# Graph-network kernel on one core: the attention stage's run masks are made once, ahead of it, and loaded per block

## The chip, the cores and the metric

One core of one Trainium2 chip runs the whole program. The metric is the device time of one execution in microseconds (us). The engines are named as in the profile: PE (TensorE), DVE (VectorE), ACT (ScalarE), POOL (GpSimd) and SP (SyncE, here only a queue that issues transfers).

## The reference, cut to what matters

Four graph layers follow one another, each with a residual and a layer norm. The change is in the fourth, an attention layer over 200,000 edges that are sorted by their target node:

```python
h = x @ W
alpha = h[dst] @ wa[:c] + edge_attr @ wa[c:c + ce] + h[src] @ wa[c + ce:]
alpha = jnp.where(alpha > 0, alpha, NEG_SLOPE * alpha)
m = jax.ops.segment_max(alpha, dst, num_segments=n)
a = jnp.exp(alpha - m[dst])
s = jax.ops.segment_sum(a, dst, num_segments=n)
out = jax.ops.segment_sum((a / (s[dst] + 1e-16))[:, None] * h[src], dst, num_segments=n) + bias
```

`dst` is sorted, so the edges of one node are a run of neighbours. The maximum over a node's edges is a running maximum that starts anew at the head of each run and is read at its last element. That needs two masks for each edge: is it the head of a run (then a term of -1e30 is added to what was carried along), and is it the last of a run (then its value is kept).

## The kernel before, in words

**Tiling.** The 6,250 nodes are 49 blocks of 128. The edges of one target block `d` lie in 49 cells of up to 128 edges, one for each source block. A cell is a column of [128, 49] tiles, or a row of [49, 128] tiles after a transpose. An earlier stage writes to DRAM the one-hot matrices of the edges' ends (`OND`, `OSD`), the dense 6250 x 6250 adjacency `AD` and, in `ROWS3`, the local source and target numbers of each cell.

**Stages.** After a first stage of some 1,240 us come the *dense passes* (`passes_*`): twice through the 49 rows of `AD`, 1.57 MB each, through three buffers, with 49 matmuls a row. POOL has no code there. Then come `pairs3_*`, the third layer, and `pairs4_*`, the attention stage. Each engine's order is what the code writes; semaphores alone tie the engines together.

**The attention stage** is a software pipeline of 343 steps `t` (7 for each block, `G` = 7), and 42 more to drain. `due4(t, off)` gives the step that work with an offset is due for, `block4(t, off)` the block when one begins. In each step:

- PE multiplies 7 cells of one-hot sources by node rows (L1668), ACT copies the result to `H` (L1606).
- ACT scales 7 cells by the attention weights (L1627, seven activations: the *values*) into one of four buffers `V4`. DVE subtracts the bf16 part (L1817), POOL subtracts the next one (L1655: the *look*). PE adds up the three parts (L1688). ACT may fill the buffer again after that.
- DVE makes one-hot rows of loaded target numbers (L1755) and source numbers (L1750), each every second step.

Once in each block there is a chain through all engines that finds the maxima:

- PE transposes the block's target numbers (L1695) into `ps[2]`; ACT copies them to `dcol` in `MISC` (L1613).
- POOL makes the masks of them in four dependent instructions on [49, 128]: difference to the neighbour (L1646), equal or not (L1648), `negs` (L1650) and `lastf` (L1651). They stand in POOL's order between two looks, so the next look waits for them.
- DVE scans with `negs` (L1841) and multiplies by `lastf` (L1843). PE transposes the product and `lastf` (L1708, L1709). DVE splits it (L1849 to L1854), PE spreads it to the edges (L1719), DVE finds the maximum of each node (L1859 to L1872), PE collects it (L1678), DVE makes the exponents (L1807 to L1813) and ACT the exponential (L1617).

Every seventh block begins a layer norm of seven finished blocks, one DVE instruction (L1771 to L1796) in each of 14 steps.

SP issues the loads: sources (L1546), targets (L1552, which wait for PE's L1678 of a block since that frees their buffers) and one-hot matrices (L1564).

Of the kernel before, what the change touches and what calls it, by code (L numbers as in the profile page):

```python
# [53 lines left out]
def gnn_kernel(nc, x, src, dst, eattr, ew, ew2, W1n, b1n, W1r, Wl1, bl1, W2n, b2n, W2r, Wl2, bl2,  # L54
               W2g, b2g, dcoef, cpar, spar, W3, watt, bias3, out):
    with ExitStack() as ctx:
# [1167 lines left out]
        def pairs3_sp(sp):  # L1224
# [14 lines left out]
            sp.wait_ge(row_mm.at, 2 * NB)  # L1239
            for n in range(4):  # L1240
# [256 lines left out]
        seg, negs, lastf, ylast = (Tflat[0:NB, 1225 + 130 * n:1225 + 130 * n + w] for n, w in enumerate((129, P, P, P)))  # L1497
# [19 lines left out]
        dtr, dcp, flg, sgk = on(cat_t, NB), on(cat_ev, NB), on(cat_d, NB), on(t_out, NB)  # L1517
# [73 lines left out]
        def pairs4_act(act):  # L1591
# [6 lines left out]
            for t in range(LASTT):  # L1598
                d, g, k = due4(t, 1)
                if k is not None:  # L1600
                    act.wait_ge(hg.at, hg.o + k + 1)
# [885 lines left out]
```

## Time and profile before

| | |
|---|---|
| median of 3 runs | 3592.72 us (3590.33 to 3595.03) |
| profiled execution | 3591.77 us, of which the span of its instructions 3590.0 us |
| PE / DVE / ACT / POOL busy, share of the span | 81% / 81% / 62% / 44% |
| first pass over `AD`, second pass | 1241 to 1461 us, 1461 to 1712 us |
| attention stage, from the first block's exponents to the last one's | 2717.7 to 3556.9 us |
| granted TensorE clock, mean | 0.94 of full speed |

A line of a group gives the line of the code, the engine, what is written and read, and the time. A time in brackets is idle time just ahead of an instruction, with what ended it. The busy time of an engine includes time in which an instruction has started and is held up, so a long duration of an instruction that is short elsewhere is itself a wait.

### The profile page before, as it was taken

What the parts mean: (1) busy time and instruction counts of PE and PEld (TensorE: products, weight loads), DVE (VectorE), ACT (ScalarE), POOL (GpSimd) and SP (SyncE); (2) the same over time, 40 slices, a digit from 0 to 9 for tenths busy, and PEclk for the clock granted to TensorE, in tenths of its full rate; (3) what the DMA queues carried; (4) which work ended last, traced back from release to release, by engine and by line L of the source; (5) the groups of instructions that cost most, each with busy time, mean ns of one, the idle gap of its engine ahead of it and who ended that gap; (6) DMA issues with size and microseconds to landing.
All of it is one profiled execution on the core that took longest, in us unless ns stands there. A gap on an engine that the chain in (4) does not pass through costs nothing.

```text
span 3590.0 us, 122167 instructions
## 1 busy us (share of the span) xinstructions
PE 2911.7 (81%) x50473; PEld 2637.4 (73%) x50473; DVE 2904.2 (81%) x4610; ACT 2219.8 (62%) x6003; POOL 1584.4 (44%) x1253
## 2 busy tenths in 40 slices
PE   0199999999999699899688888787768888888886
PEld 0178888888888599899677777777757777777775
DVE  7599999999999522233688888898857999999997
ACT  6334444444444400001698888898857898899887
POOL 2012222222221000000399988898964655666564
PEclk9999999999999899999899999999977888888887
DMA  8157777777777799898687877787738888888884
GB/s 221 66 157 244 237 232 234 243 237 231 234 243 236 253 370 360 330 328 320 215 279 259 264 264 248 254 271 250 257 124 302 279 278 277 276 290 274 267 278 129
DMA packets 606666, 907.43 MB, mean 253 GB/s; under 512 B 358505, under 2 KB 494858, under 8 KB 587163
## 3 DMA queue, kind: packets, MB, share of 16 engines
q1 hardware_dynamic: 583992, 800.62, 68.1%
q10 hardware_dynamic: 19763, 94.38, 7.1%
q8 instruction: 406, 6.65, 0.7%
q0 software_dynamic: 2352, 4.52, 0.3%
q14 instruction: 153, 1.25, 0.1%
HBM read 651.96 MB, written 247.40 MB: 251 GB/s over the span
## 4 chain that ended last, share of the span: by engine, by line
PE 36%; DVE 27%; ACT 14%; issue 10%; POOL 6%; DMA 5%; ACTq 1%; SPq 0%; DVEq 0%; POOLq 0%
PE ps L683 9%; PE ps L1047 8%; PE ps L709 4%; DMA U<-AD 4%; ACT U L1627 3%; POOL EDG L1268 3%; DVE EDG L1755 3%; DVE U L1817 3%; PE ps L696 3%; ACT U L569 3%; POOL EDG L1260 2%; ACT U L1329 2%; PE ps L667 2%; PE ps L1289 1%; DVE A L1389 1%
## 5 line engine op out<-in xcount | busy, mean ns | idle before, releaser
L569 ACT ACTIVATE U<-ps 128x512 bf16<-128x512 f32 (+1 forms) x637 | 356.4, 573 | 499.5 <-PE ps L696 475.5
L1627 ACT ACTIVATE U<-U,T 128x65 f32<-128x65 f32 x1806 | 460.1, 343 | 47.7 <-PE ps L1688 42.3
L1260 POOL TENSOR_TENSOR EDG<-U,edge 128x512 f32<-128x512 f32 (+1 forms) x196 | 214.3, 1098 | 584.1 <-DVE edge L1412 551.1
L1047 PE MATMUL ps<-U 128*128 128x192 bf16 x4802 | 418.5, 248 | 33.2 <-DMA U<-AD 32.8
L1047 PEld LDWEIGHTS ps<-U 128*128 128x128 bf16 x4802 | 402.8, 98 | 42.5 <-DMA U<-AD 39.2
L1655 POOL TENSOR_TENSOR U<-U 128x455 f32<-128x455 f32 x258 | 296.4, 1152 | 215.3 <-DVE U L1817 215.3
L866 DVE TENSOR_TENSOR EDG<-edge,EDG 128x1792 bf16<-128x1792 bf16 x343 | 367.5, 1083 | 14.4 <-DMA OSD<-EDG 12.0
L502 POOL DMA_INDIRECT U<-REC,nod x49 | 94.0, 1918 | 622.4 <-PE ps L638 501.2
L683 PE MATMUL ps<-U 128*128 128x98 bf16 (+1 forms) x5292 | 363.5, 223 | 4.5 <-DVE U L854 3.5
L709 PE MATMUL ps<-EDG,U 128*128 128x193 bf16 x2401 | 311.4, 249 | 51.1 <-ACT U L569 39.9
L683 PEld LDWEIGHTS ps<-U 128*128 128x128 bf16 x5292 | 341.3, 98 | 15.7 <-DVE U L854 11.9
L1296 PE MATMUL ps<-U 128*128 128x65 bf16 x7203 | 287.2, 195 | 72.3 <-DVE A L1389 71.8
L1270 POOL TENSOR_TENSOR EDG<-EDG 128x896 f32<-128x896 f32 (+1 forms) x172 | 312.4, 1817 | 13.5
L1268 POOL TENSOR_TENSOR EDG<-EDG 128x896 f32<-128x896 f32 (+1 forms) x172 | 308.6, 1794 | 11.7 <-ACT EDG L1348 11.7
L1296 PEld LDWEIGHTS ps<-U 128*128 128x128 bf16 x7203 | 252.1, 98 | 80.5 <-DVE A L1389 80.1
L1289 PE MATMUL ps<-U 128*128 128x65 bf16 x7203 | 289.6, 195 | 13.8 <-ACT U L1331 8.0
L1389 DVE TENSOR_TENSOR A<-ps,U 128x455 f32<-128x455 f32 x343 | 210.4, 622 | 95.7 <-ACT U L1339 77.0
L1289 PEld LDWEIGHTS ps<-U 128*128 128x128 bf16 x7203 | 271.3, 98 | 18.5 <-issue 10.1
L1348 ACT ACTIVATE EDG<-U,edge 128x64 f32<-128x64 f32 x1029 | 279.3, 338 | 9.0 <-PE ps L1308 6.1
L1139 DVE TENSOR_REDUCE A<-ps 128x64 f32<-128x192 f32 x98 | 34.3, 355 | 294.3 <-PE ps L1047 294.0
L854 DVE TENSOR_TENSOR U<-U 128x3920 bf16<-128x3920 bf16 (+1 forms) x132 | 263.7, 2000 | 0.0
L1381 DVE TENSOR_SCALAR U<-U,iotap 128x1792 bf16<-128x1792 bf16 x228 | 252.7, 1109 | 1.5 <-DMA U<-ROWS 1.5
(323 smaller groups left out, 7019.4 us busy)
## 6 DMA issues: line engine op xcount, KB each, us to landing
U<-ROWS SPq DMA_DIRECT2D x411, 448.0 KB, 4.7
U<-AD SPq DMA_DIRECT2D x98, 1568.0 KB, 8.6
OND<-EDG SPq DMA_DIRECT2D x343, 224.0 KB, 2.8
OSD<-EDG SPq DMA_DIRECT2D x343, 224.0 KB, 3.6
AD<-U ACTq DMA_DIRECT2D x49, 1568.0 KB, 5.6
EDG<-ROWS SPq DMA_DIRECT2D x171, 448.0 KB, 6.3
U<-OND SPq DMA_DIRECT2D x303, 224.0 KB, 5.9
U<-OSD SPq DMA_DIRECT2D x213, 224.0 KB, 4.7
```

Of the source, the lines that this page charges most:

```text
L569: ev4.by(act.activation(prow[i % NPW][:, P * g:P * (g + m)], ps[4 + gg % 2][:, 0:P * m], ACT.Copy))
L683: ins = pe.matmul(ps[3][:, o:o + NB * (f1 - f0)], w_, FR[h][:, c, f0:f1, :, k], start=(h + c + k + f0 == 0), stop=(last and f0 == 0))
L709: ins = pe.matmul(ps[6][:, 0:XW], prow[i % NPW][:, P * j:P * j + P], Xs[:, j, :], start=(j == 0), stop=(j == NB - 1))
L866: hot8.by(dve.tensor_tensor(HOT[r].rearrange("p s c (r k) -> p (s c) r k", k=2), bc(r1v.unsqueeze(1), [P, 14, D, 2]), bc(sdb[i % 2][:, b, ...
L1047: ins = pe.matmul(ps[q][:, 0:192], arow[r][:, P * j:P * j + P], (XsB if p else XsA)[:, j, :, :].rearrange("p s f -> p (s f)"), start=(j == ...
L1260: ins = pool.tensor_tensor(VD[:, v:v + w, 0, KA * D:G * D].rearrange("p w (k f) -> p w k f", f=D), W_, bc(c_.unsqueeze(3), [P, w, G - KA, ...
L1268: rem3.by(pool.tensor_tensor(VD[:, v:v + w, 1, :], VD[:, v:v + w, 0, :], VH[:, v:v + w, 0, :], ALU.subtract))
L1270: low3.by(pool.tensor_tensor(VD[:, v:v + w, 2, :], VD[:, v:v + w, 1, :], VH[:, v:v + w, 1, :], ALU.subtract))
L1289: ins = pe.matmul(ps[h][:, 65 * k:65 * k + 65], rw[r][:, 2 * P * k + P:2 * P * k + 2 * P], Ws[:, i0 + k, s_, 0:65], start=(s_ == 0), stop= ...
L1296: ins = pe.matmul(ps[2 + h][:, 65 * k:65 * k + 65], rw[r][:, 2 * P * k:2 * P * k + P], Ws[:, j, s_, 0:65], start=(s_ == 0), stop=(s_ == 2))
L1627: ins = act.activation(V4[k % NV][:, 0, c, :], H[k % NHR][:, c, :], ACT.Copy, scale=a4[d % 2][:, s:s + 1])
L1655: look.by(pool.tensor_tensor(V4[k % NV][:, 2, :, :], V4[k % NV][:, 1, :, :], S4[k % NV][:, 1, :, :], ALU.subtract))
```

## The change

The masks don't depend on the layers' values, only on the edges' targets. So POOL now makes them in the dense passes (`passes_pool`), for seven target blocks in one go. SP first loads all target numbers into `EDG` (49 x 49 cells of 128 numbers of two bytes, 0.61 MB), ahead of the first row of `AD`. POOL makes both masks in bf16 in `EDG`; SP stores them to a DRAM tensor `MSK` in the second pass, seven stores, each ahead of the last row of `AD` of a group. In the attention stage SP loads `MSK[d]` (49 rows of 512 bytes) into one of two buffers `masks`, behind a wait that the block two before has been read. The four POOL instructions, the ACT copy and the PE transpose of each block are gone, with their waits. The transpose of `lastf` is now a bf16 matmul with an identity. `GV` and `GR` are empty, so `value_at` and `rest_at` wait as before.

```diff
+        def passes_pool(pool):
+            msk_d.by(pool.memset(mdif[:, :, 0:1], 1.0))
+            msk_d.by(pool.memset(mdif[:, :, P:P + 1], 1.0))
+            pool.wait_ge(msk_ld.at, msk_ld.o + 16)
+            for g in range(NGB):
+                bl = slice(GB * g, GB * g + GB)
...
+                msk_d.by(pool.tensor_tensor(mdif[:, :, 1:P], mdst[:, bl, 1:P], mdst[:, bl, 0:P - 1], ALU.subtract))
+                pool.wait_ge(msk_d.at, msk_d.o + 4 * g + 3)
+                msk_d.by(pool.tensor_scalar(mdif, mdif, 0.0, 1.0, ALU.is_equal, ALU.subtract))
+                pool.wait_ge(msk_d.at, msk_d.o + 4 * g + 4)
+                msk_ok.by(pool.tensor_scalar(mboth[:, bl, 0, :], mdif[:, :, 0:P], BIG, None, ALU.mult))
+                msk_ok.by(pool.tensor_scalar(mboth[:, bl, 1, :], mdif[:, :, 1:P + 1], -1.0, None, ALU.mult))
+            pool.wait_ge(msk_st.at, msk_st.o + 16 * NGB)
+
         def passes_sp(sp):
+            msk_ld.by(sp.dma_start(mdst, ROWS3[1].rearrange("d (s r) -> s d r", r=P)), 16)
             for p in range(2):
                 for i in range(NB):
                     r = i % NA
+                    if p and i % GB == GB - 1:
+                        g = i // GB
+                        sp.wait_ge(msk_ok.at, msk_ok.o + 2 * g + 2)
+                        msk_st.by(sp.dma_start(MSK[GB * g:GB * g + GB].rearrange("d s m r -> s d (m r)"),
+                                               mboth[:, GB * g:GB * g + GB, :, :].rearrange("p d m r -> p d (m r)")), 16)
...
+            def run_masks(d):
+
+                if d >= 2:
+                    sp.wait_ge(ytr.at, ytr.o + d - 1)
+                mk_ld[d % 2].by(sp.dma_start(masks[d % 2], MSK[d]), 16)
+
             sp.wait_ge(att.at, NGB)
             nt = 0
+            run_masks(0)
+            run_masks(1)
...
+                d = block4(t, 2)
+                if d is not None and d >= 2:
+                    run_masks(d)
...
         def pairs4_act(act):
...
-                d = block4(t, 6)
-                if d is not None:
-                    act.wait_ge(dtr.at, dtr.o + d + 1)
-                    if d:
-                        act.wait_ge(flg.at, flg.o + 2 * d)
-                    dcp.by(act.activation(dcol, ps[2][0:NB, P:2 * P], ACT.Copy))
...
         def pairs4_pool(pool):
             for t in range(LASTT):
-                d = block4(t, 7)
-                if d is not None:
-                    pool.wait_ge(dcp.at, dcp.o + d + 1)
...
-                    sgk.by(pool.tensor_tensor(seg[:, 1:P], dcol[:, 1:P], dcol[:, 0:P - 1], ALU.subtract))
-                    pool.wait_ge(sgk.at, sgk.o + 2 * d + 1)
-                    sgk.by(pool.tensor_scalar(sege, seg, 0.0, 1.0, ALU.is_equal, ALU.subtract))
-                    pool.wait_ge(sgk.at, sgk.o + 2 * d + 2)
-                    flg.by(pool.tensor_scalar(negs, sege[:, 0:P], BIG, None, ALU.mult))
-                    flg.by(pool.tensor_scalar(lastf, sege[:, 1:P + 1], -1.0, None, ALU.mult))
                 d, g, k = due4(t, 18)
...
         def pairs4_pe(pe):
...
-                    dtr.by(pe.transpose(ps[2][0:NB, P:2 * P], E3v[:, d, :, 1], ident[:, :]))
...
-                    ytr.by(pe.transpose(ps[3][:, 64:64 + NB], lastf, ident[0:NB, 0:NB]))
+                    ytr.by(pe.matmul(ps[3][:, 64:64 + NB], masks[d % 2][:, 1, :], identh, start=True, stop=True))
...
         def pairs4_dve(dve):
...
-                    dve.wait_ge(flg.at, flg.o + 2 * d + 2)
-                    dvf.by(dve.tensor_tensor_scan(ysc, negs, ps[2][0:NB, 0:P], -BIG, ALU.add, ALU.max))
+                    dve.wait_ge(mk_ld[d % 2].at, mk_ld[d % 2].o + 16 * (d // 2 + 1))
+                    dvf.by(dve.tensor_tensor_scan(ysc, masks[d % 2][:, 0, :], ps[2][0:NB, 0:P], -BIG, ALU.add, ALU.max))
...
+                passes_pool(pool)
                 pairs3_pool(pool)
```

On POOL, in the middle of the attention stage, two blocks stand in a row like this before. `U<-U` and `MISC<-MISC` are looks, the 49-row instructions make masks:

```order
L1655 TENSOR_TENSOR U<-U 128x455 x3
L1655 TENSOR_TENSOR MISC<-MISC 128x455
L1646 TENSOR_TENSOR T<-MISC 49x127
L1648 TENSOR_SCALAR MISC<-T 49x129
L1650 TENSOR_SCALAR T<-MISC 49x128
L1651 TENSOR_SCALAR T<-MISC 49x128
L1655 TENSOR_TENSOR U<-U 128x455 x3
L1655 TENSOR_TENSOR MISC<-MISC 128x455
```

The same place of the changed program (the look is line L1695 there):

```order
L1695 TENSOR_TENSOR U<-U 128x455 x3
L1695 TENSOR_TENSOR MISC<-MISC 128x455
L1695 TENSOR_TENSOR U<-U 128x455 x3
L1695 TENSOR_TENSOR MISC<-MISC 128x455
L1695 TENSOR_TENSOR U<-U 128x455 x3
```

Nothing stands between two looks any more.

On SP, the dense passes were 98 loads of `AD` in one stretch, with the loads of the next stage behind them:

```order
L2397 UNCONDITIONAL_BRANCH
L999 DMA U<-AD 128x6272 x98
L1229 DMA U<-ROWS 128x1792 x8
L1237 DMA U<-OSD 128x896
L1229 DMA U<-ROWS 128x1792
```

In the changed program the same stretch begins so:

```order
L2429 UNCONDITIONAL_BRANCH
L1017 DMA EDG<-ROWS 49x49x128
L1030 DMA U<-AD 128x6272 x55
L1024 DMA MSK<-EDG 49x7x256
L1030 DMA U<-AD 128x6272 x7
L1024 DMA MSK<-EDG 49x7x256
L1030 DMA U<-AD 128x6272 x7
```

The load of all target numbers stands ahead of the first row of `AD`, and the first store of masks behind 55 rows, which is in the second pass.

On POOL, the branch was followed at once by the third layer's work, which waits for the dense passes to end:

```order
L2427 UNCONDITIONAL_BRANCH
L1260 TENSOR_TENSOR EDG<-U,edge 128x2x256 x2
L1268 TENSOR_TENSOR EDG<-EDG 128x2x448
L1270 TENSOR_TENSOR EDG<-EDG 128x2x448
L1260 TENSOR_TENSOR EDG<-U,edge 128x2x256
```

Now seven rounds of mask work stand ahead of it; the first round and the beginning of the second:

```order
L2459 UNCONDITIONAL_BRANCH
L999 MEMSET U 49x7
L1000 MEMSET U 49x7
L1008 TENSOR_TENSOR U<-EDG 49x7x127
L1010 TENSOR_SCALAR U<-U 49x903
L1012 TENSOR_SCALAR EDG<-U 49x7x128
L1013 TENSOR_SCALAR EDG<-U 49x7x128
L1006 MEMSET U 49x7
L1007 MEMSET U 49x7
```

POOL thus works at the start of the first dense pass, where it had nothing to do.

## Rows read from the trace of the kernel before

**Rows 1.** Busy time of each engine in three stretches; the header names the columns

```profile
core 0: us, PE busy (x) PEld busy (x) DVE busy (x) ACT busy (x) POOL busy (x), PEclk, DMA share, GB/s
1241.00:1461.00 220.00, 200.83 (x2351) 194.99 (x2352) 66.73 (x145) 15.02 (x32) 0.00 (x0) 0.97 0.93 359
1461.00:1712.00 251.00, 235.19 (x2578) 223.80 (x2575) 80.91 (x205) 19.68 (x66) 0.00 (x0) 0.99 0.86 315
2717.70:3556.90 839.20, 691.35 (x14102) 634.57 (x14100) 786.37 (x1782) 751.37 (x2787) 503.51 (x522) 0.87 0.83 273
```

**Rows 2.** One line's instructions, L1807, once a block: ns min/median/max, first and last start

```profile
L1807 DVE TENSOR_REDUCE ps<-ps x49: 417/462/472, 2717.7 to 3556.9; 128x98 f32<-128x294 f32 x49
```

**Rows 3.** Chain of work that ended last, 3156 to 3190: start, us, what

```profile
3169.81 1.42 DVE A L1750
...
3186.13 1.47 PE ps L1678 x49
3187.60 1.18 PE ps L1688 x7
```

**Rows 4.** Who waited for whom, 2900 to 3500 us: total, times, longest

```profile
ACT U L1627 <- PE ps L1688: 27.7, 25, 2.2
...
DVE U L1817 <- ACT U L1627: 10.7, 10, 2.1
...
DVE EDG L1755 <- DMA EDG<-ROWS: 3.1, 6, 0.9
```

**Rows 5.** Four DVE instructions and L1613 on ACT, by line: ns min/median/max

```profile
L1817 DVE TENSOR_TENSOR MISC<-MISC x85: 615/620/1869, 2729.5 to 3566.9; 128x455 f32<-128x455 f32 x85
...
L1750 DVE TENSOR_SCALAR A<-A,iotap x70: 631/709/1508, 2691.3 to 3528.9; 128x1792 bf16<-128x1792 bf16 x69, 128x896 bf16<-128x896 bf16 x1
...
L1755 DVE TENSOR_SCALAR EDG<-EDG,iotap x172: 442/681/2770, 2702.9 to 3553.2; 128x1792 bf16<-128x1792 bf16 x171, 128x896 bf16<-128x896 bf16 x1
...
L1859 DVE TENSOR_REDUCE ps<-ps x49: 300/305/311, 2714.3 to 3553.5; 128x49 f32<-128x147 f32 x49
...
L1613 ACT ACTIVATE MISC<-ps x49: 261/272/281, 2698.3 to 3537.7; 49x128 f32<-49x128 f32 x49
```

**Rows 6.** Timeline of POOL in three blocks: start, us, instruction

```profile
3166.84 0.78 POOL L1646 TENSOR_TENSOR T<-MISC 49x127 f32<-49x127 f32 x1
...
3169.32 0.52 POOL L1651 TENSOR_SCALAR T<-MISC 49x128 f32<-49x128 f32 x1
3169.81 0.94 POOL L1655 TENSOR_TENSOR U<-U 128x455 f32<-128x455 f32 x1
...
3079.39 0.94 POOL L1651 TENSOR_SCALAR T<-MISC 49x128 f32<-49x128 f32 x1
...
3081.21 0.93 POOL L1655 TENSOR_TENSOR U<-U 128x455 f32<-128x455 f32 x1
```

**Rows 7.** Timeline of DVE in the same blocks and two others

```profile
3167.29 0.81 DVE L1755 TENSOR_SCALAR EDG<-EDG,iotap 128x1792 bf16<-128x1792 bf16 x1
...
3169.73 1.50 DVE L1750 TENSOR_SCALAR A<-A,iotap 128x1792 bf16<-128x1792 bf16 x1
...
3183.54 0.82 DVE L1817 TENSOR_TENSOR U<-U 128x455 f32<-128x455 f32 x1
...
3185.99 1.52 DVE L1817 TENSOR_TENSOR U<-U 128x455 f32<-128x455 f32 x1
...
3079.86 2.77 DVE L1755 TENSOR_SCALAR EDG<-EDG,iotap 128x1792 bf16<-128x1792 bf16 x1
...
3192.35 0.93 DVE L1755 TENSOR_SCALAR EDG<-EDG,iotap 128x1792 bf16<-128x1792 bf16 x1 [0.36 <-DMA EDG<-ROWS]
```

**Rows 8.** SP's issues of the target loads, ns min/median/max, and their time to landing

```profile
L1552 SPq DMA_DIRECT2D EDG<-ROWS x172: 319/424/2037, 2696.6 to 3543.6; - x172
...
DMA to landing us min/median/max: 3.4/6.3/8.6
```

**Rows 9.** Timeline of all engines at the start of the dense passes

```profile
1241.20 18.99 SPq L999 DMA_DIRECT2D U<-AD  x5
...
1248.15 1.35 DVE L1134 TENSOR_TENSOR U<-A,U 128x448 bf16<-128x448 f32 x2
...
1248.75 13.49 PE L1047 MATMUL ps<-U 128*128 128x192 bf16 x127 [14.78 <-DMA U<-AD]
```

**Rows 10.** The page: a costly POOL group, and an issue of small pieces with us to landing

```profile
L1268 POOL TENSOR_TENSOR EDG<-EDG 128x896 f32<-128x896 f32 (+1 forms) x172 | 308.6, 1794 | 11.7 <-ACT EDG L1348 11.7
...
OND<-EDG SPq DMA_DIRECT2D x343, 224.0 KB, 2.8
```

More of the change, by code:

```diff
@@ L81, in gnn_kernel @@
         ENDS = dram("ENDS", (2, EP), I32)
+        MSK = dram("MSK", (NB, NB, 2, P), BF16)
         U = sb("U", [P, 20800])
@@ L1239, in pairs3_sp @@
             sp.wait_ge(row_mm.at, 2 * NB)
+            sp.wait_ge(msk_st.at, msk_st.o + 16 * NGB)
             for n in range(4):
@@ L1496, in cell @@
             return rows[k // 2 % n][:, e:e + P]
-        seg, negs, lastf, ylast = (Tflat[0:NB, 1225 + 130 * n:1225 + 130 * n + w] for n, w in enumerate((129, P, P, P)))
+        ylast = Tflat[0:NB, 1615:1615 + P]
+        masks = [MISC[0:NB, 1365 + P * i:1365 + P * i + P].bitcast(BF16).rearrange("p (m r) -> p m r", m=2) for i in range(2)]
+        identh = ident[0:NB, 0:NB].bitcast(BF16).rearrange("p (r h) -> p r h", h=2)[:, :, 1]
         ysc = ps[3][0:NB, P:2 * P]
@@ L1516, in gnn_kernel @@
         hg, hev = on(r_used, NG), on(pj_t, NB)
[L1517 removed]
+        mk_ld = [on(ad_st[0], 16 * ((NB + 1) // 2)), on(ad_st[1], 16 * (NB // 2))]
+        vop, rop = on(cat_t, NB), on(cat_ev, NB)
         zok, ztr, ylok, ytr = on(coef, NB), on(coll, NB), on(p3_t, NB), on(p3_ev, NB)
@@ L1533, in due4, with value_at, rest_at @@
             return (k // G, k % G, k) if 0 <= k < NT else (None, None, None)
+        GV, GR = (), ()
+        def value_at(eng, k):
+            d, g = k // G, k % G
+            if g in GV:
+                eng.wait_ge(vop.at, vop.o + d * len(GV) + GV.index(g) + 1)
+            else:
+                eng.wait_ge(vok.at, vok.o + d * (G - len(GV)) + sum(h not in GV for h in range(g + 1)))
+        def rest_at(eng, k):
+            d, g = k // G, k % G
+            if g in GR:
+                eng.wait_ge(rop.at, rop.o + d * len(GR) + GR.index(g) + 1)
+            else:
+                eng.wait_ge(rok.at, rok.o + d * (G - len(GR)) + sum(h not in GR for h in range(g + 1)))
         def block4(t, off):
@@ L1618, in pairs4_act @@
                 d, g, k = due4(t, 16)
-                if k is not None:
+                if k is not None and g not in GV:
                     act.wait_ge(exo.at, exo.o + d + 1)
@@ L1814, in pairs4_dve @@
                 d, g, k = due4(t, 17)
-                if k is not None:
-                    dve.wait_ge(vok.at, vok.o + k + 1)
+                if k is not None and g not in GR:
+                    value_at(dve, k)
                     rok.by(dve.tensor_tensor(V4[k % NV][:, 1, :, :], V4[k % NV][:, 0, :, :], S4[k % NV][:, 0, :, :], ALU.subtract))
@@ L1839, in pairs4_dve @@
                         dve.wait_ge(ytr.at, ytr.o + d)
-                    dve.wait_ge(flg.at, flg.o + 2 * d + 2)
-                    dvf.by(dve.tensor_tensor_scan(ysc, negs, ps[2][0:NB, 0:P], -BIG, ALU.add, ALU.max))
+                    dve.wait_ge(mk_ld[d % 2].at, mk_ld[d % 2].o + 16 * (d // 2 + 1))
+                    dvf.by(dve.tensor_tensor_scan(ysc, masks[d % 2][:, 0, :], ps[2][0:NB, 0:P], -BIG, ALU.add, ALU.max))
                     own()
-                    ylok.by(dve.tensor_tensor(ylast, ysc, lastf, ALU.mult))
+                    ylok.by(dve.tensor_tensor(ylast, ysc, masks[d % 2][:, 1, :], ALU.mult))
                 d = block4(t, 11)
```

27 lines of the change are left out of this document (11 added, 16 removed).

## The prediction, made before the changed kernel was run

> **What bounds the kernel now.** I read the stretches first, since the change touches two stages only. Between the exponents of the first block and those of the last lie 839.2 us and 48 blocks [rows 2], 17.5 us a block. In that stretch DVE is busy 786 us and ACT 751 us [rows 1]: 16.4 and 15.65 us a block, so DVE has 1.1 us idle and ACT 1.8 us. PE has 14.4 and POOL 10.5 us a block. DVE comes first, ACT close behind. Then I read the chain of waits over two blocks. It stays on DVE almost throughout; it leaves DVE at the end of a block's chain, by way of PE's collecting (1.47 us) and adding up (1.18 us) to ACT [rows 3]. The list of waits says the same from the other side: in 600 us DVE waits 10.7 us for ACT's values and 3.1 us for target loads, while ACT waits 27.7 us (in `U` alone) for PE to free a value buffer, which stands behind a look of POOL [rows 4].
>
> Then I asked what DVE's busy time is made of. The subtraction L1817 takes 0.62 us in the median and up to 1.87; the one-hot rows take 0.71 (L1750) and 0.68 us (L1755) in the median, and up to 1.51 and 2.77. The reduction L1859, which reads PSUM, takes 0.300 to 0.311 us in all 49 blocks [rows 5]. The instructions are the same each time, so the rest is a hold. The timelines beside each other say by whom: the L1755 that starts at 3079.86 ends at 3082.63, and on POOL the mask instruction L1651 begins at 3079.39, two looks follow, and the last ends at 3082.14 [rows 6, 7]. The rows show no overlap of the two engines on such instructions that costs nothing: DVE and POOL take turns.
>
> **A rule beside it.** The Trainium skill ("SBUF — State Buffer", section "Who interferes with whom") says that DVE instructions in a two-port mode or with two SBUF inputs share a port pair with GpSimd, as an exclusive lock for a whole instruction. By it each mask instruction could hold DVE for all of its time; four of them, some 2.7 us a block, would be worth 130 us in 49 blocks. The rows say less, since much of the mask work runs beside L1859 to L1872, which aren't held. The sum below goes by the rows.
>
> **The change, part by part.**
>
> *POOL's masks, gone.* They fill POOL from 3166.84 to 3169.84 in the block shown (four instructions) and the next look follows at once, late [rows 6]. What DVE loses by it I take from three blocks [rows 7], each against the medians [rows 5]. First block: L1755 0.81 for 0.68 and L1750 1.50 for 0.71, 0.92 us. Second: L1817 0.82 and 1.52 for 0.62, 1.10 us. Third: L1755 2.77 for 0.68, 2.09 us. The mean is 1.37. In the third, one of the two looks would have met L1755 anyway, so I take 1.2 us a block, 49 x 1.2 = 58.8 us. Bounds: if the late look merely holds DVE earlier instead, one collision with it (1.37 us instead of 0.68 is the size of a usual one, between the median and the maximum of L1750) comes back, and 0.5 us a block is left, 25 us. Above, 2.1 us a block, 103 us.
>
> *What stops it.* ACT works 15.65 us a block; less the copy L1613 (0.27 us) [rows 5] it is 15.4 us. So no more than 2.1 us a block, about 100 us, can be had whatever DVE does. The copy itself is worth nothing while DVE is ahead. Next late is the target load: it is issued only after PE's L1678 of a block and lands after 3.4 to 8.6 us [rows 8]. DVE already waits 0.36 us for one at 3192.35 [rows 7]. When DVE gets there earlier by 1.2 us, this wait grows. It binds in every second block only, where the buffer freed by L1678 is needed one step sooner. I charge another 0.36 us in 24 blocks, 8.6 us back.
>
> *PE.* One transpose of 128 columns goes, and the one of `lastf` gets cheaper. PE has 3 us idle a block; nothing.
>
> *The mask loads.* 49 more issues on SP, 0.32 us each by the shortest row of a like issue [rows 8]. A mask load is issued some seven steps ahead of the scan, 15 us at over 2 us a step; the slowest target load took 8.6 us. Behind it on SP wait one-hot loads that are many steps early. Nothing, except at the stage's start, where two of them stand ahead of the first source load: +0.6 us. The wait for `ytr` is for a block long past.
>
> *The load of the target numbers,* 0.61 MB ahead of row 0 of `AD`. PE waited for that row until 1248.75, the issue being at 1241.20 [rows 9], so all of the load is on the path. At the stage's 359 GB/s [rows 1] it is 1.7 us, the lower bound. The upper bound is by a store of 224 KB that takes 2.8 us to land [rows 10]: 614 KB by that scale, 7.7 us. I take 4. The Trainium skill ("DMA: Bandwidth & Descriptors", section "Specifications") asks for at least 512 bytes a piece for full rate, and these pieces have 256, which speaks for the upper half; no row here shows that load.
>
> *POOL's work in the passes.* Seven rounds of four instructions on 896 to 903 elements. By L1268, 1.8 us at 896 elements [rows 10], at most 7.2 us a round and 50 us in all: done long before the first store in pass two. But it begins while DVE splits the nodes' rows for PE's first row; the last split ends at 1249.5 [rows 9], and DVE has to take turns with instructions of 1.8 us. Until then five or so splits remain; between none held and all, 0 to 9 us, mostly beside the later arrival of row 0. I take +1. DVE's norms in pass one are held too, but DVE is busy only 67 of 220 us there [rows 1].
>
> *Stores of masks.* 1.2 MB in pass two, where the transfers take 0.86 of the time and PE 235 of 251 us [rows 1]: nothing.
>
> **Sum.** -58.8 + 8.6 + 0.6 + 4 + 1 = -44.6 us. The profiled execution takes 3591.8 us, so 3547.2; the median of the runs is 0.9 us above it: 3548 us.
>
> **The rivals.**
>
> 1. *More than the sum (0.15).* The late look also delays PE's sum and so ACT. If all goes with the masks, only ACT's 15.4 us a block remain: 3593 - 100 + 6 = 3499 us; half way, 3520. For it: the 27.7 us that ACT waits for PE. Against: in the chain that wait appears only at block ends.
> 2. *The target loads or ACT take it back (0.15).* If the median landing time of 6.3 us [rows 8] holds DVE in each block, 0.5 us or less is left of 1.2: 49 x 0.4 = 20, less 6: 3579 us. For it: the wait is already there; transfers already take 0.83 of the time, and a shorter block makes that more. Against: only 3.1 us in 600 so far.
> 3. *Nothing (0.07).* The masks' time lies wholly beside unheld DVE work and the looks collide as often as ever: 3586 to 3600 us.
> 4. *Slower (0.13).* Issue order decides who holds whom, and it is reshuffled. POOL is free at once for each look, which then starts just as DVE starts L1755 or L1750. If each of the 7 such instructions of a block met a look, at +0.7 us each, it would be 4.9 us a block; at present the held ones are a minority by the medians, say 2. That would be +2.9 - 1.2 = +1.7 us a block, 3593 + 83 + 6 = 3680 us. It decides from 1.7 more collisions a block on. The same section of the Trainium skill says that issue order decides who blocks; the trace agrees, since the same L1755 is short in one block and long in another.
>
> **How the numbers follow.** The forecast of the sum has 0.5: 3548 us, with 25 to 75 us won in the stage, 3525 to 3575 us. Eight in ten reach into rival 1 half way and over rival 2: 3510 to 3584 us. A measurement of this kernel tells about 0.2%, 7 us, from no change. Faster than that: 0.5 + 0.15 + 0.15 = 0.80. Within: 0.07. Slower: 0.13.
>
> **What would show it.** Right: 16.4 us or less between two L1807 where it was 17.5; no DVE instruction of 2.7 us; L1755's mean and L1817's down; ACT's wait for L1688 down; first matmul of the passes at about 1253 instead of 1248.75, second pass unchanged; more waiting of L1755 for its load. Wrong: as many holds of 1.4 us or more on L1755 and L1750 as before (rivals 3 and 4), a wait of the scan for its mask, or PE's first row held by the splits beyond 1260.

## The result, and the profile after

| | before | changed |
|---|---|---|
| median of the runs | 3592.6 us (3590.3 to 3595.0) | 3569.4 us (3566.9 to 3573.4) |
| profiled execution | 3591.8 us | 3570.8 us, span 3568.7 |
| first to last of the 49 sums L1807, now L1839 (48 blocks) | 839.2 us | 813.0 us |

The ratio is 0.9936 [0.9919, 0.9954]: 23 us faster, half of the 44.6 forecast. The line numbers have moved: L1750 is now L1782, L1755 L1787, L1817 L1849, L1807 L1839, L1627 L1682, L1688 L1728, L1678 L1718, L1606 L1667, L1668 L1708, L1655 L1695. The same stretches as in [rows 1], with the same columns:

```profile
1241.00:1465.00 224.00, 202.79 (x2401) 198.06 (x2401) 70.04 (x146) 12.96 (x28) 70.59 (x40) 0.97 0.92 355
1465.00:1712.00 247.00, 230.38 (x2521) 219.22 (x2522) 79.42 (x201) 19.54 (x65) 0.00 (x0) 0.99 0.89 325
2722.50:3535.50 813.00, 681.57 (x14054) 630.28 (x14052) 735.38 (x1781) 743.35 (x2740) 382.11 (x334) 0.86 0.85 284
```

In the attention stage DVE's busy time fell from 786.4 to 735.4 us. That is the release of the hold, 51.0 us in 48 blocks or 1.06 us a block. POOL lost 121 us of work. But the stretch shortened by 26.1 us alone, so DVE stands idle 25 us longer than before, and now ACT, at 743 us, is the busiest engine. The lines in that stretch show both (busy, mean ns, then the idle time ahead), before first:

```profile
L1817 DVE TENSOR_TENSOR U<-U 128x455 f32<-128x455 f32 x251 | 186.2, 745 | 20.1 <-ACT U L1627 18.7
L1755 DVE TENSOR_SCALAR EDG<-EDG,iotap 128x1792 bf16<-128x1792 bf16 x167 | 159.4, 955 | 5.4 <-DMA EDG<-ROWS 5.4
L1750 DVE TENSOR_SCALAR A<-A,iotap 128x1792 bf16<-128x1792 bf16 x65 | 63.0, 969 | 0.5 <-issue 0.2
```

```profile
L1849 DVE TENSOR_TENSOR U<-U 128x455 f32<-128x455 f32 x251 | 176.5, 706 | 29.7 <-ACT U L1682 27.3
L1787 DVE TENSOR_SCALAR EDG<-EDG,iotap 128x1792 bf16<-128x1792 bf16 x167 | 123.1, 737 | 17.9 <-DMA EDG<-ROWS 17.8
L1782 DVE TENSOR_SCALAR A<-A,iotap 128x1792 bf16<-128x1792 bf16 x65 | 58.2, 895 | 0.4
```

The mean of L1787 is 0.74 us where it was 0.955, and its longest, by its own line, is 1.47 where it was 2.77 [rows 5]:

```profile
L1787 DVE TENSOR_SCALAR EDG<-EDG,iotap x172: 443/681/1467, 2707.4 to 3531.8; 128x1792 bf16<-128x1792 bf16 x171, 128x896 bf16<-128x896 bf16 x1
```

The waits of the stretch, of ACT and DVE (us in total, times, longest), before first:

```profile
ACT U L1627 <- PE ps L1688: 42.3, 38, 2.5
DVE U L1817 <- ACT U L1627: 18.7, 18, 2.1
ACT MISC L1627 <- PE ps L1688: 16.0, 10, 3.4
...
DVE EDG L1755 <- DMA EDG<-ROWS: 5.4, 9, 1.8
```

```profile
ACT U L1682 <- PE ps L1728: 42.8, 43, 3.1
DVE U L1849 <- ACT U L1682: 27.3, 37, 2.1
ACT MISC L1682 <- PE ps L1728: 18.2, 12, 3.2
DVE EDG L1787 <- DMA EDG<-ROWS: 17.8, 15, 3.7
```

Before, DVE waited 5.4 us for target loads and 19.2 us for values in the same 48 blocks; now it is 17.8 and 29.4 us. ACT waits 61.0 us for a value buffer, where it was 58.3. One late load, as the timelines of SP and DVE show it:

```profile
3008.99 0.97 SPq L1602 DMA_DIRECT2D EDG<-ROWS  x2
...
3015.90 0.69 DVE L1787 TENSOR_SCALAR EDG<-EDG,iotap 128x1792 bf16<-128x1792 bf16 x1 [3.69 <-DMA EDG<-ROWS]
```

SP issues two target loads as soon as PE's L1718 has given the buffers back, and DVE stands for 3.7 us before a load that was issued 7 us ago. SP's own waits for L1718 are 123.9 us in 48 times: it isn't SP that is late, but the buffer.

The start of the passes:

```profile
1238.40 0.36 SPq L1017 DMA_DIRECT2D EDG<-ROWS  x1
1238.82 21.38 SPq L1030 DMA_DIRECT2D U<-AD  x5
...
1245.63 2.81 DVE L1165 TENSOR_TENSOR U<-A,U 128x448 bf16<-128x448 f32 x2
...
1246.30 1.66 POOL L1008 TENSOR_TENSOR U<-EDG 49x889 f32<-49x889 bf16 x1 [8.15 <-DMA EDG<-ROWS]
1248.05 3.54 POOL L1010 TENSOR_SCALAR U<-U 49x903 f32<-49x903 f32 x1
1250.28 11.96 PE L1078 MATMUL ps<-U 128*128 128x192 bf16 x127 [18.22 <-DMA U<-AD]
1251.67 2.47 POOL L1012 TENSOR_SCALAR EDG<-U 49x896 bf16<-49x896 f32 x1
```

From the first issue to PE's first matmul it is 11.9 us, where it was 7.55 [rows 9]: +4.3. One pair of DVE's splits is held by POOL, and is done before PE starts. The passes end 3.5 us later after their first issue than before.

The two profiled executions differ by 21.0 us, which add up so: the passes start 2.8 us earlier and take 3.5 us more, from their last matmul to the stage's first sum it is 4.1 us more, the 48 blocks take 26.2 us less and what follows them 0.4 us more.

### The profile page after: what moved, and what is told of

Its sections match the earlier page's. It is cut to its first block, busy times and chain, and to the rows that moved or that the text cites. A ratio compares the mean times of both kernels' runs of the same rounds, so it can differ in the third digit from the quotient of the medians.

```text
span 3568.7 us, 121778 instructions
## 1 busy us (share of the span) xinstructions
PE 2903.2 (81%) x50424; PEld 2637.3 (74%) x50424; DVE 2851.9 (80%) x4608; ACT 2211.9 (62%) x5954; POOL 1535.5 (43%) x1099
## 4 chain that ended last, share of the span: by engine, by line
PE 38%; DVE 23%; ACT 15%; issue 10%; DMA 7%; POOL 7%; ACTq 1%; SPq 0%; DVEq 0%; POOLq 0%
PE ps L684 8%; PE ps L1078 8%; PE ps L710 4%; DMA U<-AD 4%; ACT U L1682 4%; POOL EDG L1300 3%; PE ps L697 3%; ACT U L570 2%; DVE U L1849 2%; POOL EDG L1292 2%; DMA EDG<-ROWS 2%; ACT U L1361 2%; PE ps L1321 2%; PE ps L1718 2%; PE ps L668 1%
## 5 line engine op out<-in xcount | busy, mean ns | idle before, releaser
L1682 ACT ACTIVATE U<-U,T 128x65 f32<-128x65 f32 x1806 | 460.3, 343 | 44.7 <-PE ps L1728 42.8
L1695 POOL TENSOR_TENSOR U<-U 128x455 f32<-128x455 f32 x258 | 304.2, 1181 | 350.6 <-DVE U L1849 350.6
L1078 PEld LDWEIGHTS ps<-U 128*128 128x128 bf16 x4802 | 401.7, 98 | 45.9 <-DMA U<-AD 43.0
L867 DVE TENSOR_TENSOR EDG<-edge,EDG 128x1792 bf16<-128x1792 bf16 x343 | 368.6, 1087 | 14.8 <-DMA OSD<-EDG 14.1
L1300 POOL TENSOR_TENSOR EDG<-EDG 128x896 f32<-128x896 f32 (+1 forms) x172 | 307.9, 1790 | 12.4 <-ACT EDG L1380 12.4
L1321 PEld LDWEIGHTS ps<-U 128*128 128x128 bf16 x7203 | 273.1, 99 | 18.1 <-issue 10.1
L494 POOL TENSOR_TENSOR X<-X,U 128x64 f32<-128x64 f32 x49 | 102.0, 2083 | 360.1 <-ACT U L551 360.1
```

Source lines behind the costliest of these rows:

```text
L867: hot8.by(dve.tensor_tensor(HOT[r].rearrange("p s c (r k) -> p (s c) r k", k=2), bc(r1v.unsqueeze(1), [P, 14, D, 2]), bc(sdb[i % 2][:, b, ...
L1078: ins = pe.matmul(ps[q][:, 0:192], arow[r][:, P * j:P * j + P], (XsB if p else XsA)[:, j, :, :].rearrange("p s f -> p (s f)"), start=(j == ...
L1300: rem3.by(pool.tensor_tensor(VD[:, v:v + w, 1, :], VD[:, v:v + w, 0, :], VH[:, v:v + w, 0, :], ALU.subtract))
L1321: ins = pe.matmul(ps[h][:, 65 * k:65 * k + 65], rw[r][:, 2 * P * k + P:2 * P * k + 2 * P], Ws[:, i0 + k, s_, 0:65], start=(s_ == 0), stop= ...
L1682: ins = act.activation(V4[k % NV][:, 0, c, :], H[k % NHR][:, c, :], ACT.Copy, scale=a4[d % 2][:, s:s + 1])
L1695: look.by(pool.tensor_tensor(V4[k % NV][:, 2, :, :], V4[k % NV][:, 1, :, :], S4[k % NV][:, 1, :, :], ALU.subtract))
```

## The experiments

Theory 1: the hold was worth what DVE's busy time says, and the five target buffers and the four value buffers (`V4`, freed by PE's L1728) took half of it back. Theory 2: ACT's own work did. Another candidate was the shorter chain of the masks, with no hold in it.

The time ahead of the attention stage differs by 12 us between profiles with the same code there (the stage's first sum starts between 2720.3 in e10 and 2732.6 in e9), and the medians have intervals of +-3 to 6 us. So each profile's own length of the 48 blocks, first to last L1839, stands beside the median. In three kernels with the same attention stage (changed, e4, e7) it was 813.0, 813.9 and 813.6 us. A stretch still belongs to one execution, and not always to one near the median: the profiled execution of e1 took 5.0 us more than its median, that of e12 4.2 more, those of e8 and e10 8.3 and 6.1 us less. So a few us between two stretches show nothing by themselves. The waits are DVE's for target loads and for values, and ACT's for value buffers.

| kernel | median us | ratio to before | 48 blocks | DVE, ACT busy | waits: loads, values, buffers |
|---|---|---|---|---|---|
| before | 3592.6 | | 839.2 | 786.4, 751.4 | 5.4, 19.2, 58.3 |
| changed | 3569.4 | 0.9936 [0.9919, 0.9954] | 813.0 | 735.4, 743.4 | 17.8, 29.4, 61.0 |
| e1 six target buffers | 3561.9 | 0.9907 [0.9891, 0.9923] | 805.1 | 724.7, 742.6 | 0, 50.4, 52.3 |
| e2 POOL dummies | 3596.2 | 1.0007 [0.9998, 1.0016] | 834.8 | 781.3, 745.9 | 10.1, 16.1, 52.6 |
| e3 ACT dummy | 3576.5 | 0.9942 [0.9927, 0.9957] | 816.1 | 734.1, 751.5 | 19.9, 33.6, 56.9 |
| e4 late load | 3569.0 | 0.9934 [0.9920, 0.9947] | 813.9 | 736.0, 743.2 | 15.4, 30.4, 56.7 |
| e5 e1, 5 value, 16 look-up buffers | 3581.0 | 0.9966 [0.9954, 0.9978] | 822.4 | 726.7, 772.9 | 0, 63.0, 0 |
| e6 e1, values on POOL | 3591.1 | 0.9995 [0.9987, 1.0004] | 831.4 | 764.1, 670.2 | 0, 41.2, 122.4 |
| e7 no mask work in the passes | 3567.8 | 0.9927 [0.9915, 0.9939] | 813.6 | 730.3, 744.7 | 19.4, 33.2, 54.8 |
| e8 e1, rests on POOL | 3558.0 | 0.9905 [0.9892, 0.9918] | 791.7 | 723.4, 741.6 | 0.7, 36.6, 41.5 |
| e9 e1, 5 value, 17 look-up buffers | 3552.6 | 0.9884 [0.9866, 0.9902] | 788.7 | 738.2, 743.8 | 0, 21.7, 0 |
| e10 e1, 16 look-up buffers | 3589.8 | 1.0000 [0.9991, 1.0010] | 828.2 | 723.3, 774.3 | 0, 76.4, 18.3 |
| e11 e9 with e8's rests | 3550.5 | 0.9878 [0.9862, 0.9894] | 793.2 | 732.4, 742.4 | 2.9, 24.6, 0 |
| e12 e9, POOL dummies | 3582.1 | 0.9970 [0.9957, 0.9983] | 824.4 | 782.6, 746.5 | 0, 15.8, 0 |

**e1_ring6: a sixth target buffer.** Its room in `T` comes from the old masks' columns; the small tiles beside it move.

```diff
-        NRL, NRW = 5, 5
+        NRL, NRW = 6, 5
-        drow2 = [... for i in range(NRL)]
+        drow2 = [... for i in range(5)] + [Tflat[:, 1190:2086].bitcast(BF16)]
```

> The changed kernel with a sixth target-row buffer, so that SyncE may issue each target load two slots earlier. Changed kernel: 3569.4 us; VectorE spends 17.8 us of the attention stretch waiting for target loads, against 5.4 in the kernel before. Theory 1 (the late target loads take back half of what the masks' removal freed): these waits fall under 3 us and the time falls by 10 to 17 us, to 3552 to 3560. Theory 2 (ScalarE is next in the queue and takes what the loads give up): the waits on the DMA fall too, but waits of VectorE on ScalarE grow by as much, and the time stays within 3 us of 3569.4. Theory 3 (the waits are DMA bandwidth, not the moment of issue): the waits stay at 15 us or more, and so does the time.

The waits for target loads are gone altogether, and DVE's waits in the stretch are:

```profile
DVE U L1849 <- ACT U L1682: 48.9, 60, 2.1
...
DVE ps L1839 <- PE ps L1718: 4.9, 6, 1.0
...
DVE MISC L1849 <- ACT MISC L1682: 1.5, 3, 0.9
```

Of 17.8 us, 8.0 came through to the stretch and 7.5 to the median; DVE's waits for values grew by 21. So the loads were late by their moment of issue and not by the rate of the transfers (theory 3). Both other theories have a share: the late loads were real, and ACT's values come next. The loads' share is short of the 10 us that theory 1 asked for.

**e2_dummy_pool: the four instructions back, on constants.** They run in `pairs4_pool` at t = 7 of each block; nobody waits for them.

```diff
+                d = block4(t, 7)
+                if d is not None:
...
+                    dk.by(pool.tensor_tensor(dseg[:, 1:P], ident[0:NB, 1:P], ident[0:NB, 0:P - 1], ALU.subtract))
...
+                    dk.by(pool.tensor_scalar(dsege, dseg, 0.0, 1.0, ALU.is_equal, ALU.subtract))
...
+                    df.by(pool.tensor_scalar(dneg, dsege[:, 0:P], BIG, None, ALU.mult))
+                    df.by(pool.tensor_scalar(dlast, dsege[:, 1:P + 1], -1.0, None, ALU.mult))
```

> The changed kernel, with the four GpSimd instructions of the old masks put back into each block of the attention stage at their old place, on constant inputs and into columns that nobody reads; nobody waits for them. If the gain came from VectorE no longer being held by them: its one-instruction means go back (target comparison from 737 to about 950 ns, source comparison from 898 to about 970, rest subtraction from 706 to about 745), VectorE is busy some 50 us more in the stretch, and the time goes back by 20 to 30 us, to 3589 to 3599. If the gain came from the shorter chain (no transpose, no copy, no flags awaited): the time stays within 5 us of 3569.4.

```profile
L1866 DVE TENSOR_TENSOR U<-U 128x455 f32<-128x455 f32 x251 | 195.2, 781 | 17.1 <-ACT U L1682 15.8
L1804 DVE TENSOR_SCALAR EDG<-EDG,iotap 128x1792 bf16<-128x1792 bf16 x167 | 131.5, 787 | 10.6 <-DMA EDG<-ROWS 10.1
L1799 DVE TENSOR_SCALAR A<-A,iotap 128x1792 bf16<-128x1792 bf16 x65 | 66.5, 1023 | 0.5 <-issue 0.2
```

These lines are L1849, L1787 and L1782 of the changed kernel; they grew by 75, 50 and 128 ns in the mean. DVE is busy 45.9 us more, the 48 blocks take 21.8 us more, and the median stands 26.8 us higher, next to before. It isn't that the looks come later: ACT's waits for buffers (52.6 us) and DVE's for values (16.1) are shorter than in the changed kernel, and what grew is the time of DVE's own instructions. The hold is nearly the whole gain of the stage; for the shorter chain of the masks, the ACT copy included, 4.4 us are left, between 834.8 and 839.2 of one profile each. The holds fell elsewhere than expected: L1799 more, L1804 less.

**e3_dummy_copy: the ACT copy back, on a constant.**

```diff
+                d = block4(t, 6)
+                if d is not None:
...
+                    dcp.by(act.activation(dcol, ident[0:NB, 0:P], ACT.Copy))
```

> The changed kernel, with a ScalarE copy of 49 x 128 put back into each block of the attention stage, at the place of the old one, from a constant into columns that nobody reads; nobody waits for it. Its own time is about 0.27 us, 13 us over 49 blocks. If ScalarE sets the pace (theory 2): the time grows by 8 to 13 us, to 3577 to 3583. If VectorE and its loads set it (theory 1): by 0 to 4 us, to at most 3573.5. It also says how much of the gain the removed copy can account for.

47 copies added 8.1 us to ACT's busy time and 3.0 us to the stretch (against 813.0; the other two with its stage give 2.2 and 2.5). The median rose by 7.1 us with wide intervals, between the two expectations. By the stretch, about a third of ACT's time comes through. Neither engine alone sets the pace.

**e4_late_load and e7_no_pass_work.** In e4 the load of the target numbers goes behind the first three loads of `AD`; in e7 the passes lose the mask work, and every block loads `MSK[0]`.

```diff
-            msk_ld.by(sp.dma_start(mdst, ROWS3[1].rearrange("d (s r) -> s d r", r=P)), 16)
...
+                    if p == 0 and i == NA:
+                        msk_ld.by(sp.dma_start(mdst, ROWS3[1].rearrange("d (s r) -> s d r", r=P)), 16)
```

> The changed kernel, with the load of all target numbers issued after the first three loads of the first dense pass and not ahead of them. If what it costs is that the first row comes later (the first matmul of the passes started 11.9 us after the first issue, against 7.55 before): the passes shorten by 3 to 4.5 us, to about 3565.5. If it costs DMA time wherever it stands, because the passes run at the rate of their loads: the time stays within 1.5 us of 3569.4.

> The changed kernel with the dense passes free of the mask work: no load of the target numbers, no GpSimd instructions but two memsets, and of the stores one of 25 KB; each block loads the same constant masks (no reset at a run's start, every edge its run's last), so the softmax is left wrong while its work and its loads keep their sizes. Changed kernel: 3569.4 us. If the mask work costs the passes what the profile of the changed kernel shows there (first matmul 4.3 us later after the first issue, passes 3.4 us longer): 3565 to 3567. If the load and the stores are free and the shift is the scatter of one profiled execution: within 1.5 us of 3569.4. The attention stretch should be as in the changed kernel within 3 us in either case.

Their passes start like this, e4 first, then e7:

```profile
1240.66 3.17 SPq L1031 DMA_DIRECT2D U<-AD  x3
...
1243.88 0.37 SPq L1021 DMA_DIRECT2D EDG<-ROWS  x1
1247.72 2.58 PE L1079 MATMUL ps<-U 128*128 128x192 bf16 x15 [13.66 <-DMA U<-AD]
```

```profile
1240.16 3.23 SPq L1013 DMA_DIRECT2D U<-AD  x3
...
1247.23 3.06 PE L1061 MATMUL ps<-U 128*128 128x192 bf16 x18 [13.58 <-DMA U<-AD]
```

Both have the first matmul 7.1 us after the first issue, where the changed kernel has 11.9: the load ahead of the first row costs 4.8 us there. From the first issue to the last matmul of the passes it was 470.2 us before, 473.7 in the changed kernel, 470.4 in e4 and 466.8 in e7. The medians (0.4 and 1.6 us lower) can't tell either from nothing.

The other profiles say more. Eleven kernels have the passes of the changed one (it, e1 to e3, e5, e6, e8 to e12): there the first matmul comes 11.7 to 13.4 us after the first issue, and the last one 471.9 to 480.3 us after it, 475.8 in the mean. That is 5.6 us more than before and 9.0 more than in e7. Since before and e7, with all but the same work in the passes, differ by 3.4 us, the cost of the new passes is some 6 to 9 us, of which 4.2 us or more are the first row's; the rest isn't separated.

**e5_ring6_nv5, e10_ring6_nhr16 and e9_ring6_nv5_17: five value buffers.** Next in line stood ACT's wait for a value buffer. A fifth needs 1365 columns. In e5 they came from two look-up buffers and one for one-hot columns; e10 has e1's four value buffers and only `NHR` changed; in e9 the small tiles move into columns of the edge table that the stage doesn't read, and 17 look-up buffers stay.

```diff
-        NHR = 18
+        NHR = 16      (e5, e10)    NHR = 17      (e9)
-        NV = 4
+        NV = 5        (e5, e9)
```

> The kernel of e1_ring6 (3561.9 us), with five value buffers for the chain of values, rests, look and spread and not four; the room comes from two of the 18 look-up buffers and one of the 17 buffers for one-hot columns, whose loads are issued one slot later. In e1 ScalarE still waits 54.7 us for the spread products to give a value buffer back, and VectorE waits 59 us for ScalarE's values. Theory 1 (once the target loads are early, this ring of four buffers is what keeps the freed VectorE time from the sum): ScalarE's wait falls to under 20 us and the time by 10 to 30 us, to 3532 to 3552. Theory 2 (ScalarE's and VectorE's own work of some 15 us a block each bounds, and the waits only move): the time stays within 4 us of 3561.9.

> The kernel of e1_ring6 (3561.9 us, 2.11 us for a ScalarE step without a wait) with 16 look-up buffers and not 18, and nothing else; four value buffers. If the 16 buffers are what cost e5 its time: the step is 2.30 us where nothing else is waited for, and the time 3572 to 3590. If they cost nothing: 3560 to 3564, and e5's loss is from its fifth value buffer or its later loads.

> Again the kernel of e1_ring6 (3561.9 us) with five value buffers, but with 17 look-up buffers and not 16, and with all 17 buffers for one-hot columns and their old load slots; the room comes from small tiles that move into columns of the edge table that this stage no longer reads. In e5 (3581.0 us, 19 slower than e1) ScalarE's waits for the spread products fell from 52 us to nothing, while a step of one copy and seven scaled copies took 2.30 us and not 2.11. Theory 1 (the 16 buffers made the copy of a group wait for ScalarE's own instruction just before it, and that hid the gain): the step is 2.11 us again, ScalarE waits under 15 us for the spread products, and the time is 3530 to 3552. Theory 2 (more groups in flight slow the other engines, whatever the buffers): 3562 to 3581.

e5 emptied the wait for buffers and yet was 19 us slower than e1. ACT's timelines in a stretch without a wait tell why, e1 first, then e10:

```profile
3057.89 0.53 ACT L1667 ACTIVATE U<-ps 128x455 f32<-128x455 f32 x1
3058.32 1.79 ACT L1682 ACTIVATE U<-U,T 128x65 f32<-128x65 f32 x7
3059.99 0.54 ACT L1667 ACTIVATE U<-ps 128x455 f32<-128x455 f32 x1
```

```profile
3051.14 0.55 ACT L1667 ACTIVATE U<-ps 128x455 f32<-128x455 f32 x1
3051.58 1.77 ACT L1682 ACTIVATE U<-U,T 128x65 f32<-128x65 f32 x7
3053.45 0.55 ACT L1667 ACTIVATE U<-ps 128x455 f32<-128x455 f32 x1
```

A step takes 2.10 us in e1 and 2.31 in e10. With 16 buffers the copy L1667 has to wait for the scaled copies just ahead of it on its own engine (`value_at(act, k - NHR)`): it starts 0.10 us after their end, where in e1 it starts 0.12 us before it. That alone cost 23.2 us of stretch and 28 of median (e10 against e1), my own mistake in e5. With 17 buffers (e9) the step is back to 2.10 us, ACT waits for no value buffer, and the stretch is 16.4 us shorter than in e1; the median is 9.3 lower. That is theory 1 once more by the waits and the step, though the time, 3552.6 us, ends just above the 3552 that it allowed. The executions of the two kernels don't overlap (3545.5 to 3557.3 us, and 3557.9 to 3566.9 for e1). DVE's busy time rose by 13.4 us against e1, with the same instructions on DVE and POOL: the engines meet at other places. e9 also moves small tiles, which no run has apart.

**e6_ring6_gv3 and e8_ring6_gr3: work of one group in seven to POOL.** The diff's empty `GV` and `GR` say where.

```diff
-        GV, GR = (), ()
+        GV, GR = (3,), ()        (e6: seven scaled copies, from ACT)
+        GV, GR = (), (3,)        (e8: the first rest subtraction, from DVE)
```

> The kernel of e1_ring6, with the seven scaled copies of one group in seven made by GpSimd in one instruction, not by ScalarE. ScalarE loses 7 of 49 copies a block, 1.8 us of its 15.5; GpSimd gets an instruction of about 1.2 us, which holds VectorE for some 0.4 us more a block (the four mask instructions of 3.3 us together held it for 1.06). If ScalarE binds after the target loads are early: the time falls by 10 to 40 us, to 3522 to 3552. If VectorE binds: it grows by up to 15 us, to at most 3577. If both are near: within 5 us of 3561.9.

> The kernel of e1_ring6, with the first rest subtraction of one group in seven made by GpSimd, not by VectorE. VectorE loses 0.65 us a block, and is held some 0.4 us more by the instruction of about 1.15 us on GpSimd. If VectorE's busy time is what counts: net 0.25 us a block, 12 us less, near 3550. If what counts is the order on ScalarE and the ring of value buffers: the longer way of that group (GpSimd takes 1.15 us where VectorE took 0.65) is in the chain, and the time stays within 4 us or grows by up to 10 us.

The stretches of e6 and e8:

```profile
2725.00:3556.40 831.40, 694.19 (x14055) 641.65 (x14053) 764.08 (x1781) 670.15 (x2404) 438.38 (x382) 0.83 0.85 277
```

```profile
2723.20:3514.90 791.70, 667.71 (x14054) 612.13 (x14052) 723.36 (x1734) 741.61 (x2740) 421.04 (x382) 0.89 0.88 291
```

e6 missed all three expectations: 29 us slower than e1. POOL worked 54.6 us more, DVE was busy 39.4 us more, and ACT, 72 us lighter, waits 122 us for value buffers. So DVE's busy time grew by 0.72 us for each us of POOL, where the mask instructions of e2 had 0.37 (45.9 of 123.4); it is 0.8 us a block, twice the 0.4 that I had expected. POOL now also stands in the chain of the values itself. So e6 doesn't say what less work on ACT would give alone; it says that at this price it is a loss. e8 moves 48 subtractions of some 0.64 us (31 us) off DVE, and DVE's busy time falls by 1.4 us: nearly all comes back as hold, at 0.8 us per us. Yet its stretch is 13.4 us shorter, and the median 3.9. Part of what lies between these two numbers may be the choice of executions: e1's profiled one lies 5.0 us above its median and e8's 8.3 us below. What the 3.9 us come from, I haven't separated, and the intervals of e1 and e8 overlap; ACT's waits for buffers and DVE's for values both fell.

**e11_ring6_nv5_17_gr3.** e9 and e8's edit together.

> The kernel of e9, with the first rest subtraction of one group in seven made by GpSimd. In e8 it brought 3.9 us (3561.9 to 3558.0), with ScalarE still waiting 41.5 us for value buffers. If VectorE is the next bound once the ring has five buffers: 5 to 15 us less than e9. If ScalarE is (its own work is some 15.5 us a block): within 4 us of e9.

2.2 us lower in the median, 4.5 us longer in the stretch: nothing on top of e9 that can be told from none. It has, with e9, the lowest time here, 0.9878 [0.9862, 0.9894] of before.

**e12_nv5_17_dummy_pool.** e2's four instructions in e9.

> The kernel of e9 (3552.6 us), with the four mask instructions of the kernel before put back on GpSimd in each block, on constants, awaited by nobody, as in e2. On the changed kernel they cost 26.8 us (e2 against the changed kernel), where VectorE was busy 50 us more. In e9 the target loads and the ring of value buffers no longer stop VectorE: it is busy 738 of 789 us of the attention stretch and waits 22 us for ScalarE. If what took back the rest of the gain were these two waits: the four instructions now cost nearly all of VectorE's 50 us, 40 to 55 us, and the time is 3592 to 3608. If the coupling to ScalarE still hides half of it: 20 to 30 us, 3573 to 3583.

The stretch grows by 35.7 us with 44.4 us more of DVE's busy time. In the changed kernel it was 21.8 of 45.9. So by these profiles, with both rings wide, 0.80 of the hold comes through and not 0.47. The median rose by 29.5 us to 3582.1, which is in the range of the other expectation (the coupling still hides half), and 2.7 above what the same instructions cost the changed kernel (26.8). The medians don't show that the wider rings let more of the hold through; only the stretches do, one execution each. Where the last 9 us stay, three blocks tell, e9 first, then the same ones of e12 (windows from one sum to the next; DVE and ACT are the third and fourth busy times):

```profile
3027.60:3044.20 16.60, 15.03 (x324) 14.06 (x323) 16.08 (x39) 16.09 (x62) 8.81 (x8) 0.91 0.90 309
3044.20:3059.00 14.80, 12.88 (x277) 11.95 (x275) 14.22 (x35) 14.77 (x57) 7.33 (x7) 0.89 0.86 290
3244.70:3260.80 16.10, 11.95 (x277) 10.74 (x274) 12.92 (x35) 16.04 (x58) 8.03 (x7) 0.94 0.94 330
```

```profile
3038.40:3056.00 17.60, 15.07 (x322) 14.19 (x321) 17.13 (x39) 16.08 (x62) 11.47 (x12) 0.89 0.89 299
3056.00:3071.60 15.60, 13.69 (x275) 12.41 (x274) 15.09 (x35) 14.87 (x56) 10.04 (x11) 0.83 0.85 276
3264.80:3280.70 15.90, 12.80 (x281) 11.61 (x279) 13.80 (x34) 15.52 (x55) 9.62 (x11) 0.93 0.90 290
```

In the even block DVE is busy but for 0.5 us in both kernels, and the block shortens by 1.0 us, as DVE's work does. In the odd one, which has fewer one-hot rows to compare, e9's ACT is busy 14.77 of 14.8 us, seven steps of 2.1 us: that block can't get shorter. In the third, which follows the norms, ACT is busy 16.04 of 16.1 us, and 0.9 us less of DVE bring nothing at all (15.9 with the masks, 16.1 without).

All 48 blocks bear it out. Number them from 0. Between e12 and e9 the 24 even blocks shorten by 19.8 us, with 21.4 us less of DVE's work, and the 24 odd ones by 16.0 with 23.0. In e9, DVE is idle for 0.7 us or less in 19 of the even blocks; in 19 of the odd ones ACT is idle for less time than DVE. And the change itself, from before to the changed kernel, shows it most clearly: the even blocks gave 21.5 us for 29.0 us less of DVE's work, the odd ones only 4.6 us for 21.9. It is in the odd blocks that the gain was lost; e9 got 16.7 us back there and 7.7 in the even ones.

## Why the prediction was half right

Each step by its own number:

- *POOL's masks, gone, -58.8 us.* Right in kind, a little large. DVE's busy time fell by 51.0 us, 1.06 us a block and not 1.2, and e2 puts 45.9 us of it back with nothing but the four instructions. That three blocks of [rows 7] came so near has luck in it: they gave 0.92, 1.10 and 2.09 us, and the 1.2 was set by hand below their mean. The Trainium skill ("SBUF — State Buffer", "Who interferes with whom") has the lock for a whole instruction, from which the prediction worked out an estimate of 130 us; here a us of mask work on POOL costs DVE 0.37 us (e2, and again e12: 44.4 of 119.9). e6 and e8 have 0.72 and 0.8 with other work.
- *What stops it, +8.6 us.* This is the term that failed. I charged 0.36 us in 24 blocks for the target loads, and nothing for ACT, since its 15.4 us a block lay below the 16.4 forecast. DVE's idle time grew by 25 us: 12.4 of it ahead of L1787, 10.2 for ACT's values. e1 takes the loads away and gets 8 us. e9 takes ACT's wait for value buffers away and gets another 16 (9 by the medians). I had read that wait as "behind a look of POOL" [rows 4] and expected it to shrink; it went from 58.3 to 61.0 us. It is a ring of four buffers round ACT, DVE, POOL and PE. ACT's limit was right on the average and wrong in the blocks: in the changed kernel DVE is the busier of the two in 18 of the 24 even blocks and ACT in 17 of the 24 odd ones, and the odd ones passed on 4.6 us of 21.9. The charge for the loads was in the right blocks, since all 15 waits of L1787 in the stretch fall into odd ones, but they are 1.2 us each and grew by 12.4 us and not by 8.6.
- *The copy on ACT, nothing.* Nearly: 2 to 3 us of stretch by e3.
- *PE, and the loads of the masks, nothing.* Right; in no profile does the scan wait for its mask. The +0.6 us at the stage's start can't be told apart: from the last matmul of the passes to the stage's first sum it was 1006.3 us before and 1006.8 to 1012.3, 1009.5 in the mean, in the thirteen kernels that load masks. Some 3 us more, against one profile, which no term had and whose cause stays open.
- *Target numbers and held splits, +4 and +1 us.* Right for the start: 4.3 us at the first matmul, and e4 and e7 give 4.8. Over the whole passes, the stores included, which I charged nothing, it is more than the 5: the 3.5 us of the one profile are at the low end, and the mean of eleven is 5.6 us above before and 9.0 above e7.
- *POOL in the passes.* Instructions of "at most 1.8 us" by L1268 [rows 10] were 1.66 to 3.54 us; a round takes 10.2 us and not 7.2. Nothing waits for them.

The measured time lies between the forecast and rival 2, which named the right mechanism ("the target loads or ACT take it back") at too high a price. That it lies in the range is partly luck: the 26 us of the stage are just above the 25 of its lower end, but that bound stood for a late look that holds DVE elsewhere, and what happened is that the hold went almost as forecast and odd blocks kept the time. Of the signs I had named, the missing 2.7 us instructions, the fallen means, the growing wait of L1787 and the first matmul came; 16.4 us between two sums (16.94) and a shorter wait of ACT for L1728 did not.

## What to carry to other kernels

Relieving the busiest engine by x us is worth x only as far as its partners can follow. Count the buffers of each ring between them, and the slots between a buffer's release and its next use, before you book the gain; here, after a gain of 26 us in the stage, widening two rings gave another 24 (17 by the medians). Compare the engines block by block and not on the average: here the same relief of DVE, some 1 us a block, shortened even blocks by 0.9 us and odd ones by 0.2. And before taking a buffer from a ring, see which instruction then waits for whom: one that waits for its own engine's last instruction costs even when nothing else is late.

## What the runs showed of the hardware

- A `tensor_scalar` on POOL over 49 x 903 numbers in f32 took 3.26 to 3.54 us, one that writes bf16 2.44 us for 896, a `tensor_tensor` of 889 from bf16 1.66 us: the kinds with one input were the slower ones. The Trainium skill ("GPSIMD Engine Reference", "Performance versus the Vector engine") gives 1.8 cycles an element at 1.2 GHz as the best case, and 2.6 for a `tensor_tensor` as the floor of two inputs. By the former 903 elements are an estimated 1.35 us, by the latter 889 are an estimated 1.93 us; the measurements, 3.26 and 1.66 us, decide.
- DVE's busy time grew by 0.37 us per us of POOL for four small instructions on 49 partitions (e2, e12), and by 0.72 to 0.80 for 128 x 455 multiplications or subtractions (e6, e8). Whether size, kind or place in the order makes the difference isn't shown: with the same instructions on both engines, DVE's busy time differs by 13.4 us between e1 and e9.
- On ACT, an instruction that waits for its predecessor's completion starts 0.10 us after it (e10); without that wait it starts 0.12 us before its end (e1). In a step of eight instructions it is 0.2 of 2.1 us.
